# Far values and maxima of two key tiles added by one pass of four 32-row matmuls

## What is computed

```python
x = x + layernorm(attention(layernorm(x)))      # 16 heads of 64, no scaling of the scores
x = x + layernorm(mixture(layernorm(x)))        # 8 experts, 2 gated per batch element
# attention: scores = q @ k.T + bias[bucket(key - query)], softmax over all 2048 keys, @ v, @ wo
# bucket: 32 buckets by distance; one value for every distance of 91 and more, on each side
```

## Time and profile before

| | |
|---|---|
| median of 3 runs | 3255.93 us (3251.97 to 3259.44) |
| the profiled execution | 3255.61 us, its span 3253.8 us |
| mean granted TensorE clock | 0.96 |
| busy PE, POOL, DVE, ACT | 2884.5, 2273.1, 1946.7, 1604.1 us |

### The profile page before, as it was taken

One profiled execution on the slowest core, in us unless ns is written; L12 is line 12 of the kernel. 1 busy time (PEld: TensorE's weight loads), 2 busy tenths in 40 slices (PEclk: granted clock), 3 DMA queues, 4 the chain that ended last, 5 costly groups with the idle time before them and its releaser, 6 DMA issues.

```text
span 3253.8 us, 58126 instructions
## 1 busy us (share of the span) xinstructions
PE 2884.5 (89%) x18988; PEld 1074.2 (33%) x18988; DVE 1946.7 (60%) x4926; ACT 1604.1 (49%) x2048; POOL 2273.1 (70%) x1033
## 2 busy tenths in 40 slices
PE   3599999999999999998999999999999999974756
PEld 1133333333333333333333333333333333322323
DVE  5465656565556655655656565656566566546676
ACT  2255555555555455555555555555554555543333
POOL 0188888887888788888888888878887888860000
PEclk9699999999999999999999999999999999986878
DMA  6000000000000000000000000000000000010000
GB/s 154 17 1 2 1 6 14 2 1 1 19 1 2 1 19 1 1 2 18 1 2 1 7 13 2 1 1 19 1 1 1 18 2 1 2 49 30 1 26 26
DMA packets 45640, 38.30 MB, mean 12 GB/s; under 512 B 21318, under 2 KB 43846, under 8 KB 45046
## 3 DMA queue, kind: packets, MB, share of 16 engines
q1 hardware_dynamic: 45302, 34.13, 4.0%
HBM read 29.17 MB, written 11.34 MB: 12 GB/s over the span
## 4 chain that ended last, share of the span: by engine, by line
PE 60%; issue 18%; DVE 12%; ACT 6%; DMA 1%; SPq 1%; DVEq 0%; ACTq 0%; POOL 0%; POOLq 0%
PE po L531 20%; PE st L501 17%; PE pre L513 6%; PE st L713 5%; PE pm L469 4%; ACT prob L764 4%; PE pm L561 3%; DVE mpart L1006 3%; PE pm L475 2%; DVE st L1023 2%; DVE pre L1003 2%; PE pm L540 1%; ACT o L797 1%; ACT qk L745 1%; DMA t_scratch<-w_scratch 1%
## 5 line engine op out<-in xcount | busy, mean ns | idle before, releaser
L441 POOL TENSOR_TENSOR acc<-acc,prob 128x1024 f32<-128x1024 f32 x896 | 2112.8, 2358 | 478.8 <-ACT prob L764 438.1
L764 ACT ACTIVATE prob<-st 128x1024 f32<-128x1024 f32 x1026 | 1017.9, 1021 | 1042.7 <-DVE st L1023 733.3
L531 PE MATMUL po<-prob,v 128*64 128x512 f32 x4096 | 992.6, 605 | 0.0
L501 PE MATMUL st<-qk 64*128 64x512 f16 x6156 | 845.6, 381 | 19.3 <-ACT prob L764 16.5
L998 DVE CUSTOM_DVE_ANT_0 pre<-pre,ew 128x512 f32<-128x512 f32 x460 | 308.9, 713 | 611.5 <-issue 611.5
L1003 DVE CUSTOM_DVE_ANT_0 pre<-pre,tab 128x512 f32<-128x512 f32 x716 | 483.9, 716 | 111.5 <-issue 110.3
L501 PEld LDWEIGHTS st<-qk 64*128 64x128 f16 x6156 | 296.3, 95 | 346.7 <-ACT prob L764 56.2
L513 PE MATMUL pre<-qk 64*128 64x512 f16 x1630 | 318.6, 388 | 87.0 <-DVE mpart L1006 35.7
L501 PE MATMUL st<-eq,ek 64*128 64x512 f16 x2052 | 394.3, 381 | 0.0
L531 PEld LDWEIGHTS po<-prob,v 128*64 128x64 f32 x4096 | 248.6, 136 | 439.6 <-issue 369.7
L1006 DVE TENSOR_REDUCE mpart<-pre 128x2 f32<-128x1024 f32 x227 | 277.8, 1224 | 120.9 <-PE pre L513 117.6
(11 more groups left out here) (142 smaller groups left out, 2466.5 us busy)
## 6 DMA issues: line engine op xcount, KB each, us to landing
t_scratch<-w_scratch SPq DMA_DIRECT2D x2, 3072.0 KB
inv_r<-inv SPq DMA_DIRECT2D x260, 1.0 KB, 1.7
y<-x SPq DMA_DIRECT2D x2, 2048.0 KB, 11.3
qk<-x SPq DMA_DIRECT2D x2, 2048.0 KB, 12.7
out<-qk SPq DMA_DIRECT2D x2, 2048.0 KB, 7.5
w<-w_pairs SPq DMA_DIRECT2D x9, 384.0 KB, 3.7
t2f<-t_scratch SPq DMA_DIRECT2D x9, 384.0 KB, 4.5
t<-t_scratch SPq DMA_DIRECT2D x8, 384.0 KB, 3.2
```

The lines of the kernel that those rows point to most:

```text
L441: nc.gpsimd.tensor_tensor(acc[g % 2][:, :, :], a, prob[:, n % RING, :, :], ALU.add).then_inc(sum_p, 1)
L501: last = nc.tensor.matmul(st[:, 2 * (n % 2) + h, :], w[64 * h:64 * h + 64, :], t[64 * h:64 * h + 64, :], start=(r == 0), stop=(r == len(te ...
L531: last = nc.tensor.matmul(po[64 * h:64 * h + 64, :], v[:, g // CHUNKS, j, 64 * h:64 * h + 64], prob[:, n % RING, h, :], start=(s == 0), st ...
L764: nc.scalar.activation(prob[:, n % RING, :, :], st[:, 2 * (n % 2):2 * (n % 2) + 2, :], ACT.Exp).then_inc(exp_done, 1)
```

## The change

The three score terms of a step stay. The fourth term leaves `scores`. A new function `score_rows` makes it for two steps and two heads at once: four matmuls of 32 rows, one in each quarter of the array, each writing one of the four banks of `st`. PE calls it after the second piece of a pair, and the `st_ready` of both steps is raised there. So that each quarter has its operands, the 9 rows of `eq` stand in four partition groups (0, 32, 64, 96) in place of two: the maxima come by four small DMAs in place of two, and `far_rows` has four instructions of 8 partitions in place of two of 32. The row of the maxima is row 8 of a group.

```diff
-M_ROW = 32
+M_ROW = 2 * QT
...
-    r = np.arange(128) % 64
+    r = np.arange(128) % 32
...
-                for h in range(2):
-                    sp.dma_start(eq[64 * h + M_ROW:64 * h + M_ROW + 1, g % 2, :].rearrange("p (t q) -> p t q", q=128),
+                for k in range(4):
+                    h = k % 2
+                    sp.dma_start(eq[32 * k + M_ROW:32 * k + M_ROW + 1, g % 2, :].rearrange("p (t q) -> p t q", q=128),
                                  mrow[QT * h:QT * h + QT, :]).then_inc(m_in, 16)
...
-                         (kl[b][:, keys], qh[b][:, queries]), (ek[:, variant(c, j), :], eq[:, g % 2, :])]
+                         (kl[b][:, keys], qh[b][:, queries])]
                 for r, (w, t) in enumerate(terms):
                     for h in range(2):
-                        last = nc.tensor.matmul(st[:, 2 * (n % 2) + h, :], w[64 * h:64 * h + 64, :], t[64 * h:64 * h + 64, :],
-                                                start=(r == 0), stop=(r == len(terms) - 1))
-                last.then_inc(st_ready, 1)
+                        nc.tensor.matmul(st[:, 2 * (n % 2) + h, :], w[64 * h:64 * h + 64, :], t[64 * h:64 * h + 64, :],
+                                         start=(r == 0), stop=False)
+
+            def score_rows(i, n):
+
+
+                g, s, _ = step_of(n)
+                if s == 0:
+                    pe.wait_ge(m_in, (i * SLOTS + n // TT + 1) * 64)
+                    if g < 2:
+                        pe.wait_ge(far_set, (i + n // STEPS) * 8 + 4 * g + 4)
+                for d in range(2):
+                    j = step_of(n + d)[2]
+                    for h in range(2):
+                        k = 2 * d + h
+                        last = nc.tensor.matmul(st[:, k, :], ek[32 * k:32 * k + 32, variant(g % CHUNKS, j), :],
+                                                eq[32 * k:32 * k + 32, g % 2, :], start=False, stop=True)
+                    last.then_inc(st_ready, 1)
...
                     next_piece(n + 1)
+                    score_rows(i, n + 2)
                     before = jobs(n, before)
...
-                for h in range(2):
-                    nc.scalar.activation(eq[64 * h:64 * h + 32, buf, :].rearrange("p (t q) -> p t q", q=128),
-                                         rowc[64 * h:64 * h + 32, 0:QT].unsqueeze(2).broadcast_to((32, QT, 128)), ACT.Copy,
-                                         scale=farv[64 * h:64 * h + 32, 0, bass.ds(2 * pair + h, 1)]).then_inc(far_set, 1)
+                for k in range(4):
+                    part = slice(32 * k, 32 * k + 2 * QT)
+                    nc.scalar.activation(eq[part, buf, :].rearrange("p (t q) -> p t q", q=128),
+                                         rowc[part, 0:QT].unsqueeze(2).broadcast_to((2 * QT, QT, 128)), ACT.Copy,
+                                         scale=farv[part, 0, bass.ds(2 * pair + k % 2, 1)]).then_inc(far_set, 1)
```

More of the change, by code:

```diff
@@ L403, in _ @@
             sp.wait_ge(sum_p, (G_ALL + 1) * SUMS)
-            sp.wait_ge(m_in, 32 * (G_ALL + 1))
+            sp.wait_ge(m_in, 64 * (G_ALL + 1))
             sp.wait_ge(lo_v, 8 * (B * PAIRS + 1))
@@ L483, in scores_wait @@
                 if s == 0:
-                    pe.wait_ge(m_in, (G + 1) * 32)
-                    if g < 2:
-                        pe.wait_ge(far_set, (i + n // STEPS) * 4 + 2 * g + 2)
                     if c == 0:
@@ L609, in _ @@
                 scores(n)
+            score_rows(0, 0)
             for u in range(AHEAD):
@@ L955, in far_rows @@
             def far_rows(pair, buf):
[L958 to L961, removed]
+                for k in range(4):
+                    part = slice(32 * k, 32 * k + 2 * QT)
+                    nc.vector.tensor_scalar(eq[part, buf, :].rearrange("p (t q) -> p t q", q=128),
+                                            rowc[part, 0:QT].unsqueeze(2).broadcast_to((2 * QT, QT, 128)),
+                                            farv[part, 0, bass.ds(2 * pair + k % 2, 1)], None, ALU.mult).then_inc(far_set, 1)
             def pair_table(pair, k):
```

## The result

| | before | after |
|---|---|---|
| median | 3256.05 us (3251.97 to 3259.44) | 3427.02 us (3422.47 to 3430.41) |
| ratio | | 1.0525 (1.0507 to 1.0543) |
| span of the profiled execution | 3253.8 us | 3420.6 us |

What follows compares the result with a forecast made beforehand. TensorE, 89% busy, was taken as first bound, with second pieces now waiting for the first's maximum. Eight slots' delays sum to 15.1 us, times 8 iterations 121, on 3255.6: 3377 us, chance 0.54, range 3320 to 3440.

Steps and rivals of the forecast that it cites:

- Second piece waits, pair costs L + 0.31 + 0.31: Each pair's second piece waits for the first's maximum or relu (L, 1.55 to 1.90 us); before, 1.95 + 0.31.
- (b): Rival: the pass of four tiles needs no switch from the pieces, 45 us less, 3332 us; chance 0.18.
- (c): Rival: the pass's four weight loads don't overlap, 0.19 more in seven pairs of eight, 3462 us; chance 0.10.
- (e): Rival: delays vanish in waits that were taken for full, time within 0.2%; chance 0.03.
- the estimate from the Trainium skill's 3.07 times: Four 32-row tiles gain 3.07 times, not 4: pass 30% longer, 0.07 us, about 30 us more in sum.
- (a): Rival: the wait for the first piece's maximum doesn't bite, PE keeps 0.12 a pair, 3194 us; chance 0.05.
- Slot 2, +1.65: The slot worked out pair by pair, from late second pieces and a late band, gets 1.65 us longer.
- 1.5 for slots 1 and 5, 1.45 for slot 4: Us added per slot by slot 2's rules, with earlier lateness forgotten at step 4, where PE already waits for DVE.
- GpSimd starts its sums up to a few us later and has 7 us of air: GpSimd's later sums fit its idle time in each slot and were costed at nothing.
- Slot 0, 4.3: Four far-value activations on ACT make step 6's second piece 2.92 us late; with later passes the slot grows 4.3.
- (d): Rival: PE's clock falls more often after waits, 15 us in eight more slots, 109 in 56 others, 3392 to 3486; chance 0.10.
- nothing stands behind them that PE needs soon: In slot 7 the far-value activations delay nothing PE needs soon; the slot was forecast 1.75 us longer.

Runs made afterwards that it cites:

- the best version: The changed kernel with the pass of four ahead of the second piece in every pair and far values in two instructions: 3308.0 us, 1.0163.

## Why the forecast was right in sign and 50 us short

- **Second piece waits, pair costs L + 0.31 + 0.31:** right. The pieces are 1.57, 1.79 and 1.90 apart for "less", "single" and "near" (forecast 1.55, 1.77, 1.90). The pass is 0.33 long and starts 0.32 behind the piece. Rivals (b), no switch, and (c), serial weight loads, fall with these two numbers, and (e), delays that vanish, with the 171 us. So does the estimate from the Trainium skill's 3.07 times (TensorE: Matmul & The Clock Gate, Measured speedup vs the span model): of its 0.07 no more than 0.02 is to be seen beyond the 0.31 to 0.32 that the 4-row matmul's neighbours had shown.
- **Rival (a), faster:** wrong at its point. No pair has its pieces 1.52 apart. The version with the pass ahead showed further that the saving on PE exists only behind the piece, where one of the two switches was paid already.
- **Slot 2, +1.65:** +1.48. Its pairs are longer by 0.05, 0.07, 0.28, 0.17, 0.45, 0.49, 0 and -0.04. PE's second piece of step 10 waits 1.47 there, where about 2 was forecast.
- **"1.5 for slots 1 and 5, 1.45 for slot 4 (my reading of where PE's waits stand, good to 0.2)":** this step failed. They got 3.16, 2.68 and 2.34 longer, which is 3.73 x 8 = 30 of the missing 50 us. I carried slot 2's list over and didn't ask what DVE has queued in the other slots. In slots 0, 1, 4 and 5 a copy of the projection stands behind step 8's exps on ACT, and its second half on DVE ahead of the next reduce. Slot 1 before, timeline:

```profile
1252.09 0.60 ACT L745 ACTIVATE qk<-pm 128x512 f16<-128x512 f32 x1
1252.73 0.69 DVE L984 SCALAR_TENSOR_TENSOR qk<-pm,qk 128x512 f16<-128x512 f32 x1 [1.31 <-ACT qk L745]
...
1253.01 0.39 PE L513 MATMUL pre<-qk 64*128 64x512 f16 x2
...
1253.51 1.23 DVE L1006 TENSOR_REDUCE mpart<-pre 128x2 f32<-128x1024 f32 x1
```

  and after:

```profile
1313.95 0.97 DVE L1040 TENSOR_TENSOR st<-st,t 128x768 f32<-128x768 f32 x1 [0.81 <-PE st L514]
...
1315.11 1.94 ACT L779 ACTIVATE prob<-st 128x1024 f32<-128x1024 f32 x2 [4.42 <-DVE st L1040]
...
1317.12 0.39 PE L526 MATMUL pre<-qk 64*128 64x512 f16 x2
...
1317.57 0.69 DVE L1001 SCALAR_TENSOR_TENSOR qk<-pm,qk 128x512 f16<-128x512 f32 x1 [1.31 <-ACT qk L760]
1318.18 1.22 DVE L1023 TENSOR_REDUCE mpart<-pre 128x2 f32<-128x1024 f32 x1
...
1319.45 0.39 PE L526 MATMUL pre<-qk 64*128 64x512 f16 x2 [0.65 <-DVE mpart L1023]
```

  The reduce started 0.50 behind its piece, as soon as it can, and now starts 1.06 behind it, since the late band (1313.95) carries exps, copy and DVE's half along. PE's second piece waits 0.65. The pair of step 8 has grown from 4.45 to 5.45. For the pairs of steps 8 and 10 together the list had 1.18 (0.87 and 0.31); they are longer by 1.78 in slot 1, 1.87 in slot 4 and 2.06 in slot 5, which is 17 of the 30 us. Another 6 are `low_wo` in slot 1, the next point, and half of what is left is the pair of step 6 (0.32 in slots 1 and 5, where 0.13 was taken). The pair of step 8 in slot 1 shrinks to 5.13 with the pass ahead at step 6 alone, and to 4.51 with it ahead at both steps.
- **"GpSimd starts its sums up to a few us later and has 7 us of air":** the cost of nothing failed in one place. The air is there, but the lateness moved a sum onto `low_wo`: 0.78 an iteration. The Trainium skill says why (SBUF — State Buffer, Who interferes with whom): a DVE instruction with two inputs in SBUF shares a port with a GpSimd instruction that reads SBUF, and whoever is second stands still for the whole of the other. The 2.58 beside 0.42 agree.
- **Slot 0, 4.3:** 5.59. The place is right. After the change:

```profile
1260.49 2.93 ACT L786 ACTIVATE eq<-rowc,farv 8x512 f16<-8x512 f32 x4
...
1264.17 0.69 DVE L1001 SCALAR_TENSOR_TENSOR qk<-pm,qk 128x512 f16<-128x512 f32 x1 [4.40 <-ACT qk L760]
1264.78 1.21 DVE L1023 TENSOR_REDUCE mpart<-pre 128x2 f32<-128x1024 f32 x1
...
1266.05 0.39 PE L526 MATMUL pre<-qk 64*128 64x512 f16 x2 [2.62 <-DVE mpart L1023]
```

  The forecast wait of over 2 us is 2.62, and the pieces are 4.30 apart. What I had left out of the sum is rival (d), right for this slot: PE's clock. Stretches (us; busy PE, PEld, DVE, ACT, POOL; clock), first slots 0 and 6, then the pairs of steps 6 and 8 of slot 0 in this iteration and in another:

```profile
1244.69:1293.69 49.00, 43.50 (x266) 13.88 (x267) 25.53 (x64) 25.23 (x32) 36.46 (x17) 0.97 0.01 2
1517.33:1567.18 49.85, 43.67 (x339) 17.26 (x339) 28.64 (x68) 23.72 (x29) 35.64 (x17) 0.97 0.01 2
```

```profile
1261.75:1276.24 14.49, 11.66 (x66) 3.37 (x65) 8.20 (x17) 5.83 (x10) 7.67 (x5) 0.88 0.01 0
531.06:544.53 13.47, 10.01 (x65) 3.08 (x64) 8.12 (x17) 5.83 (x10) 7.66 (x5) 1.00 0.01 0
```

  For a while after its wait PE stands at the lower level, 1.2 GHz, in seven of the eight iterations. In one, the second stretch, the same wait of 2.62 leaves the clock at 2.4 GHz. That iteration shows what the clock costs. The pair of step 6 lasts 8.22 there and 9.86 elsewhere, the pair of step 8 lasts 5.25 and 4.62, since PE waits less in it for its second piece: 1.0 us net, 7 us in all. In slot 6 the pair of step 12, behind the long wait, is 0.53 longer at a mean grant of 0.66 in place of 0.73, another 4 us. So the clock took more in the slots in which the forecast named a long wait, 0 and 6, 11 us where (d) had 15 for slot 0 alone. It was no case of its own for "up to half of the slots" but a term that belonged in the sum.
- **Slot 7, "nothing stands behind them that PE needs soon":** right, its middle is 1.91 longer. But its last pair went from 6.92 to 7.87 (means of seven): from the last value matmul over the loop's jump to the first piece of the next iteration. These are the 7 waits "issue" above, 13.7 and now 20.7 us, 18.1 with the far values in two, 27.2 with the pass ahead at step 8, and 9.9 in the version with 64-row matmuls behind the piece. They follow no edit that I can name. Some 7 us of the 50 stand there. Their cause stays open.

By slots, the missing 50 us are 30 in slots 1, 4 and 5 (the failed step, with `low_wo`), 10 in slot 0 (7 of them the clock), 9 in slot 7 (7 of them the loop's jump) and 5 in slot 6 (4 of them the clock), less 5 that slots 2 and 3 were counted too high. That 3427 still lies under the forecast's upper end of 3440 is partly luck: the room above 3377 was left for (d) and a part of (c), and what filled most of it was neither.

Of the pairs' own sources, experiments show 71 us for the place of the pass in the pairs of steps 6 and 8, 41 for its place in the other six, and 8 to 15 for the far values. Why 52 us remain with the best version is shown only in part. The first tile of a pair still completes 0.4 later, and the pair of step 10, mean of all slots, is 0.2 to 0.3 longer (47.71 against 45.81 over eight slots with the pass ahead). A version that keeps each tile's own pass of rows for its own `st_ready` and still has four tiles wasn't tried; it would be a pass of two tiles again.

## What to carry to other kernels

Packing small matmuls of two tiles into one pass saves TensorE time only if the pass costs less, with its switches, than what it replaces: here 0.42 for 0.43 us among 64-row matmuls, and 0.33 for 0.43 where one of the switches was there already. It also ties both tiles' completion to the later one, so look at who waits for the first tile before counting the passes. If a list of delays is worked out for one stage of a schedule, redo it for each stage with another queue of work behind the delayed instruction: that carried-over list was the largest part of the error. When a delayed engine "has air", check what its instructions will now run beside.

## What the runs showed of the hardware

- Four 32-row matmuls of 512 columns in the four quarters start within 0.01 us of each other (one row of x4, 0.39 us with latency). In a stream they take 0.33 to the next work, of which 0.11 is the switch; no time of their four weight loads is to be seen in that.
- `low_wo`, an element-wise instruction of VectorE with all operands in SBUF, took 0.42 us where it ended 0.1 behind a GpSimd sum's start, and 1.33 or 2.58 us beside a GpSimd sum, and two `tensor_scalar` of 0.24 each took 2.49 us. Two activations of ScalarE into SBUF beside the same sum took 1.12 together and were not held. VectorE's instructions with an operand in PSUM (L1001, L1040) kept their 0.69 and 0.97.
- The same wait of 2.62 us in the same place was followed in seven iterations by a stretch of 14 us with a mean grant of 0.88, and in one by a stretch with 1.00. The low clock cost 1.64 us in its pair and 1.0 in all, as the next pair was 0.63 shorter.
- PE's idle time at the loop's jump varied between 9.9 and 27.2 us over 7 jumps among kernels that differ only in the order of matmuls or in far values.
